# Two fp16 parts of Wo and of the state in the output projection, and five buffers for gathered rows

## The reference, cut to what matters

```python
def step(carry, xs):                       # xattn, 128 steps
    r, state = carry
    r = decay * r + kt * vt
    retained = (qt * r).reshape(B, D)
    inp = retained @ Wi.T + bi
    gate = sigmoid(inp @ Wg.T + bg)
    blended = gate * state + (1.0 - gate) * inp
    state = tanh(blended @ A.T + inp @ Bm.T)
    out = state @ Wo.T + bo                # the product that the change touches
...
x = x + tanh(g_xattn) * xattn(layernorm(x), ctx, ctx, ...)
x = x + tanh(g_ffn) * ffn(layernorm(x), ...)   # swiglu; w_shared; top 2 of 8 experts
```

## Time and profile before

| what | value |
|---|---|
| median of 3 runs | 502.77 us (500.86 to 505.42) |
| profiled execution, its own time | 503.73 us |
| its span | 502.0 us |
| TensorE busy / weight loads | 437.6 us (87%) / 355.7 us |
| VectorE busy | 372.6 us (74%) |
| ScalarE busy | 220.8 us (44%) |
| GpSimd busy | 180.1 us (36%) |
| mean granted TensorE clock | 0.972 of full speed |

### The profile page before, as it was taken

The page is one execution under the profiler, slowest core; times in us unless marked ns, Lnnn a source line. Parts: engine busy times, 40 slices in busy tenths (PEclk is TensorE's granted clock), DMA queues, the critical chain, the costliest instruction groups (busy, mean ns, idle before and its releaser), DMA issues.

```text
span 502.0 us, 12178 instructions
## 1 busy us (share of the span) xinstructions
PE 437.6 (87%) x4344; PEld 355.7 (71%) x4344; DVE 372.6 (74%) x1318; ACT 220.8 (44%) x518; POOL 180.1 (36%) x217
## 2 busy tenths in 40 slices
PE   5987799999897889999998899989799997989761
PEld 4874678888776778888777798878576764866320
DVE  2687989789987976768978777797378566536866
ACT  3554557567554445555556364635133131232100
POOL 3012304132463713021667553325144242544710
PEclk9999899999998999999999999999899998999976
DMA  7785052241514174743231596943011095582422
GB/s 163 212 205 146 3 146 45 94 111 40 148 52 140 67 156 107 138 106 80 81 106 43 112 202 171 181 128 116 21 34 53 26 215 120 133 213 97 152 80 104
DMA packets 99531, 57.05 MB, mean 114 GB/s; under 512 B 72080, under 2 KB 90000, under 8 KB 99472
## 3 DMA queue, kind: packets, MB, share of 16 engines
q1 hardware_dynamic: 95120, 44.72, 37.3%
q0 software_dynamic: 4352, 11.54, 7.7%
HBM read 23.22 MB, written 24.51 MB: 95 GB/s over the span
## 4 chain that ended last, share of the span: by engine, by line
PE 48%; DVE 29%; issue 7%; ACT 3%; DMA 3%; POOL 3%; SPq 0%; DVEq 0%; POOLq 0%; ACTq 0%
PE bank L580 15%; PE bank L569 10%; PE bank L627 6%; PE rec L713 5%; DVE u_hi L1278 4%; PE rec L594 4%; DVE u_full L1280 3%; DMA raw_w<-hrows 2%; DVE r L1381 2%; PE rec L599 2%; PE bank L852 2%; ACT state L969 2%; DVE hs L1607 2%; PE rec L627 1%; DVE ret L1394 1%
## 5 line engine op out<-in xcount | busy, mean ns | idle before, releaser
L969 ACT ACTIVATE state<-rec 128x64 f32<-128x64 f32 x128 | 36.6, 286 | 180.0 <-PE rec L599 179.9
L1278 DVE SCALAR_TENSOR_TENSOR u_hi<-gt,state 128x64 f16<-128x64 f32 x127 | 41.9, 330 | 76.5 <-ACT state L969 76.0
L1833 POOL DMA_INDIRECT hrows<-hid_rows,slots_i x44 | 49.5, 1125 | 78.6 <-ACT state L969 47.6
L594 PE MATMUL rec<-u_hi,a_hi 128*128 128x32 f16 x512 | 47.9, 195 | 18.7 <-DVE u_hi L1278 18.5
L1846 POOL DMA_INDIRECT yg<-yrows,slots_i x44 | 45.2, 1027 | 50.6 <-ACT state L969 33.0
L594 PEld LDWEIGHTS rec<-u_hi,a_hi 128*128 128x128 f16 x512 | 37.0, 98 | 27.8 <-DVE u_hi L1278 23.6
L594 PE MATMUL rec<-u_hi,a_lo 128*128 128x32 f16 x512 | 47.5, 194 | 0.0
L580 PE MATMUL bank<-w_hi,hid_hi 128*128 128x512 f16 x80 | 32.1, 401 | 9.7 <-DVE raw_w L1299 9.1
L599 PE MATMUL rec<-u_lo,a_hi 128*128 128x32 f16 x512 | 36.4, 194 | 2.0 <-DVE u_lo L1283 1.1
L1280 DVE SCALAR_TENSOR_TENSOR u_full<-gt,state 128x64 f32<-128x64 f32 x127 | 37.8, 298 | 0.0
L1776 POOL TENSOR_TENSOR hs_lo<-hs,hs_hi 128x512 f16<-128x512 f32 x15 | 17.4, 1157 | 55.8 <-ACT hs_hi L1170 55.8
(11 more groups left out here) (291 smaller groups left out, 1408.3 us busy)
## 6 DMA issues: line engine op xcount, KB each, us to landing
x_sb<-in_x_dram SPq DMA_DIRECT2D x16, 256.0 KB, 3.3
c_sb<-in_ctx_dram SPq DMA_DIRECT2D x64, 64.0 KB, 3.2
xr_sb<-in_x_dram SPq DMA_DIRECT2D x16, 256.0 KB, 3.9
hrows<-zeros SPq DMA_DIRECT2D x4, 1024.0 KB, 6.0
yrows<-squares_w SPq DMA_DIRECT2D x16, 256.0 KB, 3.3
yrows<-squares_sh SPq DMA_DIRECT2D x15, 256.0 KB, 3.0
raw_w<-in_L_ffn_w_dram SPq DMA_DIRECT2D x8, 256.0 KB, 5.0
out_dram<-raw_w SPq DMA_DIRECT2D x8, 256.0 KB, 2.4
```

Of the source, the lines that this page charges most:

```text
L594: pe.matmul(o[:, oc, :], w[:, kc, oc * P:(oc + 1) * P], u_hi[t % 2][:, kc, :], start=False, stop=False, skip_group_check=True)
L969: act.activation(step_of(state[i % 2], t), step_of(rec[i % 2], t), ACT.Tanh, scale=1.0 / PSCALE).then_inc(st_ready, 1)
L1278: dve.scalar_tensor_tensor(out=u_hi[p][:, :, :], in0=gate, scalar=1.0, in1=old, op0=ALU.add, op1=ALU.mult).then_inc(uh_ready, 1)
L1833: pool.indirect_dma_start(hrows[q % 2], bass.IndirectOffsetOnAxis(ap=slots_i[q][:, at:at + 1], axis=0), hid_rows[t % 6][:, s, :, :].rearra ...
```

## The change

The Wo product is made of two fp16 parts of each factor, as the products of the feed-forward layer already are: high times high, high times low, low times high. Four fp32 matmuls become twelve fp16 matmuls. The state of a finished tile gets a high part (a cast on ScalarE, new, between tanh_step(i, 0) and wo_preset) and a low part (a subtraction on VectorE, new, between retained and the two small operations on the logits). TensorE waits for both. In the set-up the transposed Wo gets a low part on VectorE. The wait of tanh_step(i, 0) for `wo_done` of tile i-2 becomes one for the low part of its state. `FETCHED` is 5 in place of 6.

```diff
-FETCHED = 6
+FETCHED = 5
...
-        whole_wo = sb("whole_wo", [P, KC, D])
+        split["wo"] = (sb("wo_hi", [P, KC, D], F16), sb("wo_lo", [P, KC, D], F16))
...
+        st_s = (sb("st_hi", [P, KC, TOK], F16), sb("st_lo", [P, KC, TOK], F16))
...
                 if k.has(c):
                     pe.wait_ge(wo_bias, k.n(c))
-                    pe.wait_ge(st_ready, k.steps(c, STEPS))
+                    pe.wait_ge(st_hi, k.n(c))
+                    pe.wait_ge(st_lo, k.n(c))
                     for s in range(HALVES):
-                        for kc in range(KC):
-                            last = pe.matmul(bank[B_WO][:, s * D:(s + 1) * D], state[c % 2][:, kc, s * P:(s + 1) * P],
-                                             whole_wo[:, kc, :], start=False, stop=(kc == KC - 1), skip_group_check=True)
+                        last = token_product(bank[B_WO][:, s * D:(s + 1) * D],
+                                             lambda part, kc: split["wo"][part][:, kc, :], st_s, s, False)
...
                     if t == 0 and k.has(i - 2):
-                        act.wait_ge(wo_done, k.n(i - 2))
+                        act.wait_ge(st_lo, k.n(i - 2))
...
-                    act.wait_ge(setup_dve, 10)
-                    act.wait_ge(setup_act, 10)
+                    act.wait_ge(setup_dve, 11)
...
-            act.mul(flat(whole_wo[:, :, :]), bank[4][:, :], fold[:, 0:1]).then_inc(setup_act, 1)
+            act.mul(flat(split["wo"][0][:, :, :]), bank[4][:, :], fold[:, 0:1]).then_inc(setup_act, 1)
...
                 tanh_step(i, 0, k)
+                if k.has(c):
+                    if k.has(c - 1):
+                        act.wait_ge(wo_done, k.n(c - 1))
+                    act.wait_ge(st_ready, k.steps(c, STEPS))
+                    act.copy(flat(st_s[0][:, :, :]), flat(state[c % 2][:, :, :])).then_inc(st_hi, 1)
                 wo_preset(c, k)
...
             gated_state(0, 6, first)
+            dve.wait_ge(setup_act, 10)
+            dve.scalar_tensor_tensor(out=flat(split["wo"][1][:, :, :]), in0=bank[4][:, :], scalar=fold[:, 0:1],
+                                     in1=flat(split["wo"][0][:, :, :]),
+                                     op0=ALU.mult, op1=ALU.subtract).then_inc(setup_dve, 1)
...
                 gated_state(i, 0, k)
                 retained(a, k)
+                if k.has(c):
+                    dve.wait_ge(st_hi, k.n(c))
+                    if k.has(c - 1):
+                        dve.wait_ge(wo_done, k.n(c - 1))
+                    low(flat(st_s[1][:, :, :]), flat(state[c % 2][:, :, :]), flat(st_s[0][:, :, :]), st_lo)
```

More of the change, by code:

```diff
@@ L298, in gated_layer @@
         wo_bias = sem("wo_bias")
+        st_hi, st_lo = sem("st_hi_ready"), sem("st_lo_ready")
         wo_done, x1_ready, ln2_stats, ln2_aggr, ln2_var, ln2_rstd, ln2_shift, xn2_ready = (
```

## The result

The change makes the kernel slower: 512.12 us as the median of 4 runs (509.72 to 513.74), beside 502.93 for the kernel before (500.86 to 505.42, 4 runs). The ratio is 1.0177, 95% interval 1.0112 to 1.0241. The quotient of the two medians is 1.0183. Forecast were 509.7 us and a ratio of 1.0137. The profiled execution took 509.72 us, its span is 508.0 us and the mean granted clock 0.961; it is the fastest of the four.

A forecast was written before the change was run, and what follows sets the result against it. The prediction took VectorE's queue up to `hs`, which releases the product behind Wo, as the bound. Pushes of 5.8 us, set-up 0.60 and iteration 1's 0.55 sum to 6.9, giving 509.7 us; range 503.5 to 512.5.

The forecast's parts named there:

- TensorE's saving is worth nothing: Wo product: 0.50 us less TensorE work per tile, 8.0 over 16, gains nothing since `hs` ends the wait behind it.
- Rival A: TensorE is the bound: its 0.50 comes back in each of iterations 2 to 15, time 495.8 us; chance 0.06.
- rival D: The change misses its place: parts never late, both additions covered, nothing moves, 502.8 us; chance 0.05.
- The cast on ScalarE is hidden: State's high half, between tanh(i, 0) and wo_preset: 0.62 us fits into ScalarE's idle time, cost nothing.
- The subtraction pushes VectorE's queue by 0.60 and all of it lands where VectorE has no gap: State's low half, between `retained` and `hs`: nine iterations at 0.60 are 5.4, with iteration 12, 5.8 us.
- rival B: The push is absorbed later in VectorE's idle time; about half of the 6.9 arrives, 506 us; chance 0.17.
- TensorE's new wait is covered by 0.5: Before Wo, iteration 4: with the low half awaited, Wo ends at 118.69, while `hs` allows the next product at 119.21.
- The granted clock fell in new places: Sign that the forecast is wrong: TensorE's clock dropping where it had not before; no size given.
- The set-up: Low half of Wo on VectorE ahead of gated_state(0, 7): 0.6 to 0.73 us, taken as 0.60, all on the path.
- Iteration 1: No `hs` here; twelve Wo matmuls at half the clock take 2.62 us and end 0.55 later than before.
- Five buffers cost nothing: Tile 10's last gather goes out at 487.3, lands at 490.9 to 494.3, before VectorE wants it at 497.39.
- Rival C: The new subtraction meets GpSimd's and they lock each other out: four iterations at 1.0 each, 513.7 us; chance 0.07.

The follow-up runs named there:

- halves unused: Kernel after, with the old fp32 Wo product and no low half of Wo; both state halves still made, no product waits for them: 508.86 us, ratio 1.0109.

## Why the prediction was right

The time lay in the range, 2.4 us above the point and 0.4 below its upper end, and its likeliest case, an unabsorbed push on VectorE with TensorE's saving worth nothing, is the one that the runs show. By its steps:

*TensorE's saving is worth nothing.* Shown twice: without the subtraction the ratio is 0.9991, and with the subtraction but the old product it is 1.0109. Rival A falls with the first, rival D with the second.

*The cast on ScalarE is hidden.* It is still made in the kernel without the subtraction, which costs nothing. Shown with it: the low half of Wo is in that kernel too, and whatever it costs in the set-up (+0.68 there, +0.67 in the kernel after, against +0.11 without it) is below what its interval can tell.

*The subtraction pushes VectorE's queue by 0.60 and all of it lands where VectorE has no gap.* The kernel with the halves unused carries this almost alone: 1.0109 is 5.5 us (interval 2.7 to 8.2), the step gave 5.8. Doubling it gave more and not less, and just as much again where the clock stayed full, so it isn't absorbed, which is against rival B. Step by step, from tanh(i, 1) to tanh(i, 2), the push is within 0.11 of the forecast in eleven of the thirteen iterations from 2 to 14 in that kernel, 7 and 8 with it, where it was said to be hidden. The two others are errors of the forecast. In iteration 5 it had "no gap", but VectorE sat idle 0.29 ahead of `hs` there, and 0.24 arrived. In iteration 11 the duo was to absorb the push, and +0.36 (kernel after) and +0.93 (halves unused) were left at its end. In the kernel after the two errors cancel in the sum, -0.32 and +0.36, which is luck. What whole iterations show besides is not the push: from tanh(6, 6) to tanh(7, 0) 0.60 was won, and 0.28 lost again by tanh(7, 1), in the kernel without the subtraction as well as in the kernel after. All profiles of kernels with the cast have this, and those of the kernel before, of five buffers alone and of `hs` first in the kernel before do not; I have not traced which instruction it comes from.

*TensorE's new wait is covered by 0.5.* Right for the order of events: in iteration 4 TensorE would have been ready 0.37 before `hs` allowed the next product, and the wait is there, 11.8 us in 12 places. What the step left out is that an engine that idles longer may come back at half the clock. That is the mis-sized term: iteration 13 cost 1.81 where 0.60 was forecast, with the clock at 0.50 from 343 to 346, and the kernel without the new wait lost 0.73 there. "The granted clock fell in new places" was named as what would make the forecast wrong; it did, and 1.2 us is too little to leave the range. The doubled subtraction shows the same term several times over. That the wait is the cause is not shown: with the earlier subtraction, and a wait of 0.40, most of the spell in iteration 13 stayed, and with the doubled one, and a wait of 1.67, iteration 13 had none. What brings a spell to one iteration and not to another stays open.

*The set-up* was forecast at 0.60 and measured 0.67. *Iteration 1* was forecast at 0.55. The Wo product went as worked out: at a clock of 0.50 throughout it ended 0.10 later than before with the iteration's start 0.52 earlier, so +0.62. Of the other 0.76, 0.65 is the spell from 60 to 62 that the kernel before, with five buffers, has as well.

*Five buffers cost nothing*: 0.9995. The last gather went out at 495.08; forecast was 487.3, to which the 6.0 us belong by which the whole run is longer, so it was 1.8 later than worked out. VectorE did not wait.

*Rival C*: its mechanism is real and its price of 1.0 was about right in the kernel with the subtraction on GpSimd: 0.9 to 1.3 in seven meetings and nothing in two. In the kernel after no `st_lo` was stretched: the view of its line gives 672 to 684 ns for all sixteen.

What stays open is the difference between 1.0177 and 1.0109, the kernel after and the one with the halves unused. It is 3.4 us, of which the set-up and iteration 13 in the profiles explain 0.6 and 1.1; the intervals overlap widely, and the rest may be chance. In the one pair of profiles the stretch behind tanh(15, 0) gave 2.5 us back, which is spread between executions and no gain: there the kernel before had TensorE at a clock of 0.50 from 420 to 422 and waiting 1.7 us for a transposed read at 443.88, and the kernel after had neither.

## What to carry to other kernels

Ask of a product that is to be shortened who releases the instruction behind it; if that is another engine, shortening buys nothing, and what the shortening asks of that engine is paid wherever it has no idle time to hide it. Splitting a factor into parts moves work from TensorE to the engines that make the parts and also makes the product start later: count both. And when such a wait is found, move the awaited instruction up in its queue: here that one move, without any change of the arithmetic, was worth 0.7% (0.4 to 1.0) of the kernel before, where 8 us less work on the "bound" engine were worth nothing.

## What the runs showed of the hardware

The granted clock fell from full to 0.50 after an idle time of 1.67 us ahead of Wo (kernel with two subtractions, iteration 4) and stayed full after 1.06 us in iteration 4 of the kernel after; in iteration 13 of the same kernel it fell after 1.06, and in the kernel with the earlier subtraction it fell there with 0.40. Nor does 1.67 decide: in iterations 2, 6, 13 and 14 of the kernel with two subtractions the clock stayed full behind it. At the low level twelve fp16 matmuls of 256 columns took 2.51 us, at the full one 1.31.

The kernel before pays for subtractions on GpSimd already. Thirteen rows of `u_hi`, `u_full` or `u_lo` in its profile are stretched to 1.00 to 1.91 us, where 0.22 to 0.28 is usual, and each overlaps a subtraction on GpSimd.

The same program doesn't have its spells of low clock in the same places each time: from 60 to 62 the kernel before had 1.00 and the same with five buffers 0.50, for 1.05 us. A difference of a microsecond between two profiles is not yet an effect of a change; a third kernel that shares the stretch tells.
